# Expert weights that follow the shared weights chunk by chunk, gelu rows moved by pairs, whole-row scatter-adds

## The reference

```python
x = x + ((x*ys) @ W0) * d          # ys = cond/sqrt(512), d = rsqrt(ys^2 @ W0^2 + 1e-8); x is 4096 x 512
s = sigmoid([x, cond] @ router_W); top 2 of 8 by s + router_bias; gates = s_sel / sum(s_sel)
shared = (silu(x @ w1) * (x @ w3)) @ w2                       # hidden 1024
routed = sum over the 2 experts of gate * (gelu(x @ W1e) @ W2e)  # hidden 512
x = x + (shared + routed) / 3
```

## Time and profile before

| | |
|---|---|
| median of 3 runs | 1090.85 us (1090.34 to 1093.66) |
| the profiled execution's own time | 1096.81 us |
| its span | 1095.0 us |
| PE busy | 1036.6 us (95%) |
| DVE, ACT, POOL busy | 509.7, 293.2, 350.3 us |
| chain that ended last | PE 85%, DMA 7%, DVE 3%, issue 3% |

### The profile page before, as it was taken

How to read it: one execution, slowest core, us unless ns; L and a number is a source line. 1 busy time by engine, 2 the same in 40 slices (tenths; PEclk the granted TensorE clock), 3 DMA queues, 4 the chain that set the end, 5 groups by cost and what they waited for, 6 DMA issues and landing times.

```text
span 1095.0 us, 14421 instructions
## 1 busy us (share of the span) xinstructions
PE 1036.6 (95%) x4692; PEld 839.7 (77%) x4692; DVE 509.7 (47%) x824; ACT 293.2 (27%) x461; POOL 350.3 (32%) x320
## 2 busy tenths in 40 slices
PE   6999999999999999999999988979999999999993
PEld 5888778888888888888888876767777777777872
DVE  4555466677332433332322134545555555555642
ACT  3222252332322222222111122223332233233330
POOL 2000000001124434433314001346664454554666
PEclk9999999999999999999999999989999999999997
DMA  4667587768768776778525459978779999999764
GB/s 175 195 217 236 199 287 251 264 227 227 291 211 270 238 274 216 249 255 266 209 49 200 61 171 282 296 172 155 140 147 239 206 218 221 228 225 198 142 119 58
DMA packets 172714, 226.77 MB, mean 207 GB/s; under 512 B 29984, under 2 KB 137888, under 8 KB 163552
## 3 DMA queue, kind: packets, MB, share of 16 engines
q1 hardware_dynamic: 59168, 142.22, 39.8%
q0 software_dynamic: 35024, 46.28, 20.7%
q10 hardware_dynamic: 78464, 37.51, 14.3%
HBM read 111.01 MB, written 96.54 MB: 190 GB/s over the span
## 4 chain that ended last, share of the span: by engine, by line
PE 85%; DMA 7%; DVE 3%; issue 3%; ACT 1%; SPq 0%; POOLq 0%; POOL 0%; DVEq 0%
PE banks L525 11%; PE banks L527 10%; PE banks L526 10%; PE banks L464 10%; PE banks L463 10%; PE banks L465 10%; DMA we<-we_d 5%; PE banks L477 5%; PE banks L478 5%; PE banks L479 5%; PE banks L411 3%; PE banks L412 3%; PE banks L413 3%; DMA out<-ys,row 1%; PE banks L443 1%
## 5 line engine op out<-in xcount | busy, mean ns | idle before, releaser
L1168 POOL DMA_INDIRECT out<-ys,row x142 | 226.2, 1593 | 260.7 <-DMA out<-ys,row 137.2
L463 PE MATMUL banks<-xh,w13h 128*128 128x512 f32 x512 | 200.1, 391 | 1.8 <-DVE xl L732 1.8
L465 PE MATMUL banks<-xh,w13l 128*128 128x512 f32 x512 | 199.9, 390 | 0.0
L464 PE MATMUL banks<-xl,w13h 128*128 128x512 f32 x512 | 199.8, 390 | 0.0
L800 DVE SCALAR_TENSOR_TENSOR gm<-sil,banks 128x512 f32<-128x512 f32 x64 | 43.9, 687 | 252.1 <-ACT sil L606 252.1
L525 PE MATMUL banks<-we,xgth 128*128 x284 | 115.1, 405 | 17.5 <-issue 12.4
L606 ACT ACTIVATE sil<-banks 128x512 f32<-128x512 f32 x64 | 38.2, 597 | 320.9 <-PE banks L465 320.9
L525 PE MATMUL banks<-we,hidth 128*128 x284 | 113.2, 399 | 8.0 <-issue 7.8
L463 PEld LDWEIGHTS banks<-xh,w13h 128*128 128x128 f32 x512 | 96.6, 189 | 22.6 <-issue 2.3
L526 PE MATMUL banks<-we,xgth 128*128 x284 | 112.2, 395 | 0.0
L527 PE MATMUL banks<-we,xgtl 128*128 x284 | 112.2, 395 | 0.0
(11 more groups left out here) (156 smaller groups left out, 1462.2 us busy)
## 6 DMA issues: line engine op xcount, KB each, us to landing
we_d<-ehl SPq DMA_DIRECT2D x32, 1024.0 KB, 7.1
hturn<-hid ACTq DMA_DIRECT2D x284, 64.0 KB
xg<-xs_d ACTq DMA_DIRECT2D x136, 128.0 KB
eraw<-expert_w SPq DMA_DIRECT2D x32, 512.0 KB
we<-we_d SPq DMA_DIRECT2D x8, 2048.0 KB
we<-we_d SPq DMA_DIRECT2D x32, 512.0 KB
x1t_d<-x1t SPq DMA_DIRECT2D x8, 1024.0 KB, 8.8
xin<-x1t_d SPq DMA_DIRECT2D x8, 1024.0 KB, 9.5
```

The lines of the kernel that those rows point to most:

```text
L463: pe.matmul(ps[hc % 2][:, :], w_hi, xh[:, j, c, :], start=(c == 0), stop=False)
L464: pe.matmul(ps[hc % 2][:, :], w_hi, xl[:, j, c, :], start=False, stop=False)
L465: last = pe.matmul(ps[hc % 2][:, :], w_lo, xh[:, j, c, :], start=False, stop=(c == DC - 1))
L1168: pool.indirect_dma_start(out_half, IO(row2[:, h, t:t + 1], 0), ys[:, t % RING, h * D // 2:(h + 1) * D // 2], None, compute_op=ALU.add).th ...
```

## The change

1. `w13h` and `w13l` become one buffer `w13[hc, part]` in the same 64 KiB, so that chunk hc has high and low next to each other. Loads 1, 2, 3 and 4 then lie over chunks 0-1, 2-3, 4-5 and 6-7.
2. SP issues loads 1 to 3 as soon as chunks 1, 3, 5 of the last shared block are multiplied (and the load before has landed). Loads 4 to 7 go in parts of 0.5 MB, each waiting for the part before; the last output store stands behind load 4.
3. `move_h` moves two tiles with 4 DMAs, after the odd tile; `hturn` is [2, 4, 2, 128]. TURN_LAG goes from 2 to 3, LAG from 3 to 4. The hold-back for `o_done` is at t = 1.
4. `scatter` is one indirect DMA of whole rows. It waits for tile t-2, and for tile t-1 only when that is of another expert, or when tiles are padding; the count to wait for is a table `wait_for` that DVE works out in 7 small steps (`scatter_waits`, in place of two operations at L1095) and POOL reads into a register.

```diff
-TURN_LAG = 2
+TURN_LAG = 3
-        w13h = sb("w13h", [HC, 2, DC, P], FP32R, 16)
-        w13l = sb("w13l", [HC, 2, DC, P], FP32R, 48)
+        w13 = sb("w13", [HC, 2, 2 * DC * P], FP32R, 16)
-        hturn = sb("hturn", [RING, SUB, P], FP32, 160)
+        hturn = sb("hturn", [2, SUB, PAIR, P], FP32, 160)
...
-            sp.wait_ge(ab_done, HC * NBLK)
-            load_weight(1, first[0], slice(0, 1))
-            store_out(NBLK - 1)
-            weight_loaded(1)
-            for i in range(2, HRING):
+            for i in (1, 2, 3):
+                sp.wait_ge(ab_done, HC * (NBLK - 1) + 2 * i)
                 load_weight(i, first[i // 2], slice(i // 2, i // 2 + 1))
                 weight_loaded(i)
+            sp.wait_ge(ab_done, HC * NBLK)
+            load_in_parts(4, first[2], slice(2, 3))
+            store_out(NBLK - 1)
+            for i in range(5, HRING):
+                load_in_parts(i, first[i // 2], slice(i // 2, i // 2 + 1))
...
-            def move_h(t):
-                act.wait_ge(hid_done, t + 1 + 2)
+            def move_h(m):
+                n = min(PAIR, TILES - m * PAIR)
+                act.wait_ge(hid_done, m * PAIR + n + 2)
                 for g in range(P // Q):
-                    act.dma_start(hturn[g * Q:(g + 1) * Q, t % RING], hid[:, t % RING, g * P:(g + 1) * P]).then_inc(h_moved[t % RING], 16)
+                    act.dma_start(hturn[g * Q:(g + 1) * Q, m % 2, :, 0:n], hid[:, m % 2 * PAIR:m % 2 * PAIR + n, g * P:(g + 1) * P]).then_inc(h_moved[m % 2], 16)
...
-                    if t == 0:
+                    if t == 1:
                         act.wait_ge(o_done, SUB * NBLK)
-                    move_h(t)
+                    if t % PAIR == PAIR - 1 or t == TILES - 1:
+                        move_h(t // PAIR)
...
-                    for h in range(2):
-                        dve.wait_ge(added[h], 16 * (t + 1 - RING))
+                    dve.wait_ge(added[t % 2], 16 * ((t - RING) // 2 + 1))
...
+            def scatter_waits():
+                at, used = cst[0:1, C_TIX:C_TIX + TILES], e8[0:1, 1, E - 1:E]
+                then(dve.tensor_scalar(wait_for[0:1, :], at, 1.0, None, ALU.add))
+                then(dve.tensor_scalar(wait_for[0:1, :], wait_for[0:1, :], 1, 255, ALU.logical_shift_right, ALU.bitwise_and))
+                then(dve.tensor_tensor(same[0:1, 1:TILES], turn_of[0:1, 1:TILES], turn_of[0:1, 0:TILES - 1], ALU.is_equal))
+                then(dve.tensor_scalar(tail[0:1, :], at, used, None, ALU.is_lt))
+                then(dve.tensor_tensor(same[0:1, 1:TILES], same[0:1, 1:TILES], tail[0:1, 1:TILES], ALU.mult))
+                then(dve.tensor_tensor(same[0:1, 1:TILES], wait_for[0:1, 1:TILES], same[0:1, 1:TILES], ALU.subtract))
+                dve.tensor_scalar(wait_for[0:1, 1:TILES], same[0:1, 1:TILES], 16.0, None, ALU.mult).then_inc(waits_done, 1)
...
             def scatter(t):
+                if t > 1:
+                    pool.wait_ge(added[t % 2], 16 * (t // 2))
+                if 0 < t < 3:
+                    pool.wait_ge(added[(t - 1) % 2], 16)
+                elif t:
+                    landed = pool.value_load(wait_for[0:1, t:t + 1], min_val=16, max_val=16 * (TILES // 2 + 2))
+                    pool.wait_ge(added[(t - 1) % 2], landed)
+                    pool.sem_inc(scatter_free, 1)
                 pool.wait_ge(ys_done, t + 1 + 2)
-                for h in range(2):
-                    if t:
-                        pool.wait_ge(added[h], 16 * t)
-                    pool.indirect_dma_start(out_half, IO(row2[:, h, t:t + 1], 0), ys[:, t % RING, h * D // 2:(h + 1) * D // 2], None,
-                                            compute_op=ALU.add).then_inc(added[h], 16)
+                pool.indirect_dma_start(out[:, :], IO(slot[:, t, 0:1], 0), ys[:, t % RING, :], None,
+                                        compute_op=ALU.add).then_inc(added[t % 2], 16)
```

More of the change, by code:

```diff
@@ L109, in shared_moe_kernel @@
         xgt = sb("xgt", [2, DC, P], FP32, 192)
-        row2 = sb("row2", [2, PADDED], INT32, 196)
+        wait_for = sb("wait_for", [TILES], INT32, 196)
+        same = sb("same", [TILES], INT32, 196.5)
+        tail = sb("tail", [TILES], INT32, 197)
         x1tok = sb("x1tok", [BLK // Q, DC, Q], FP32, 168)
@@ L219, in shared_moe_kernel @@
         xgt_done, hid_done, hidt_done = sem("xgt_done"), sem("hid_done"), sem("hidt_done")
-        h_moved = [sem(f"h_moved{k}") for k in range(RING)]
+        h_moved = [sem(f"h_moved{k}") for k in range(2)]
         ys_done = sem("ys_done")
-        halved = sem("halved")
-        added = [sem(f"added{h}") for h in range(2)]
+        waits_done, scatter_free = sem("waits_done"), sem("scatter_free")
+        added = [sem(f"added{j}") for j in range(2)]
         block = ctx.enter_context(nc.Block())
@@ L326, in load_weight @@
                              we_d[bass.ds(e * 4 + i % 2 * 2, 2)].rearrange("h p s n -> p h (s n)").bitcast(FP32)).then_inc(we_in[i % HRING], 16)
+            parts_before = [16 if i < 4 else 0 for i in range(HRING)]
             def load_in_parts(i, e, place):
                 for q in range(4):
-                    sp.dma_start(we[:, bass.ds(place, 1), i % 2, q // 2, q % 2].rearrange("p a c n -> p (a c n)").bitcast(FP32),
-                                 we_d[bass.ds(e * 4 + i % 2 * 2 + q // 2, 1), :, q % 2].rearrange("a p n -> p (a n)").bitcast(FP32)).then_inc(we_in[i % HRING], 16)
-                    sp.wait_ge(we_in[i % HRING], 16 + 16 * (q + 1))
+                    sp.dma_start(we[:, place, i % 2, q // 2, q % 2].rearrange("p a c n -> p (a c n)").bitcast(FP32),
+                                 we_d[bass.ds(e * 4 + i % 2 * 2 + q // 2, 1), :, q % 2].rearrange("a p n -> p (a n)").bitcast(FP32)).then_inc(we_in[i], 16)
+                    sp.wait_ge(we_in[i], parts_before[i] + 16 * (q + 1))
+                parts_before[i] += 64
                 sp.sem_inc(weights_in, 1)
@@ L375, in _ @@
                 for i in (2 * r, 2 * r + 1):
-                    load_in_parts(i, e, place)
+                    load_in_parts(i % HRING, e, bass.ds(place, 1))
             sp.wait_ge(pads_in, 16)
             sp.wait_ge(out_stored, 16 * NBLK)
-            for h in range(2):
-                sp.wait_ge(added[h], 16 * TILES)
+            for j in range(2):
+                sp.wait_ge(added[j], 16 * ((TILES - j + 1) // 2))
         @block.tensor
@@ L461, in up @@
                     for c in range(DC):
-                        w_hi, w_lo = w13h[:, hc, m, c, :], w13l[:, hc, m, c, :]
+                        w_hi, w_lo = (w13[:, hc, k, (m * DC + c) * P:(m * DC + c + 1) * P] for k in range(2))
                         pe.matmul(ps[hc % 2][:, :], w_hi, xh[:, j, c, :], start=(c == 0), stop=False)
@@ L591, in _ @@
                 act.wait_ge(wraw_in[n % 2], 16 * (n // 2) + 16)
-                act.activation(w13h[:, n].rearrange("p m c n -> p (m c n)"), wraw[:, n % 2, :], ACT.Copy).then_inc(w_high, 1)
+                act.activation(w13[:, n, 0, :], wraw[:, n % 2, :], ACT.Copy).then_inc(w_high, 1)
             def w2_high(g):
@@ L776, in _ @@
                 dve.wait_ge(w_high, n + 1)
-                w_hi = w13h[:, n].rearrange("p m c n -> p (m c n)").bitcast(FP32)
-                dve.tensor_tensor(w13l[:, n].rearrange("p m c n -> p (m c n)"), wraw[:, j, :], w_hi, ALU.subtract).then_inc(w_split, 1)
+                dve.tensor_tensor(w13[:, n, 1, :], wraw[:, j, :], w13[:, n, 0, :].bitcast(FP32), ALU.subtract).then_inc(w_split, 1)
             def w2_low(g):
@@ L1066, in turn_h @@
             def turn_h(t):
-                dve.wait_ge(h_moved[t % RING], 16 * (P // Q) * (t // RING + 1))
+                if t % PAIR == 0:
+                    dve.wait_ge(h_moved[t // PAIR % 2], 16 * (P // Q) * (t // RING + 1))
                 if t >= 2:
@@ L1071, in turn_h @@
                 dve.transpose(hidt[:, t % 2].rearrange("p c (a r) -> p a c r", r=Q),
-                              hturn[:, t % RING].rearrange("p a (c n) -> p a c n", n=Q)).then_inc(hturn_done, 1)
+                              hturn[:, t // PAIR % 2, :, t % PAIR].rearrange("p a (c n) -> p a c n", n=Q)).then_inc(hturn_done, 1)
             def take_h(t):
@@ L1093, in _ @@
                     dve.wait_ge(slots_in, 16 * SUB)
-                    for h in range(2):
-                        dve.tensor_scalar(row2[:, h, :], slot[:, :, 0], 2.0, float(h), ALU.mult, ALU.add).then_inc(halved, 1)
+                    scatter_waits()
                 if t > LAG:
@@ L1158, in _ @@
                         load_row(m + XB)
-            pool.wait_ge(halved, 2)
-            out_half = out.rearrange("t (h d) -> (t h) d", h=2)
+            pool.wait_ge(waits_done, 1)
             def scatter(t):
-                pool.wait_ge(ys_done, t + 1 + 2)
-                for h in range(2):
-                    if t:
-                        pool.wait_ge(added[h], 16 * t)
```

(7 more changed lines are left out.)

## The result

The changed kernel takes 1099.16 us (median of 20 runs, 1093.92 to 1102.71), the kernel before 1087.26 (20 runs, 1078.42 to 1093.66). The ratio is 1.0101, with a 95% interval of 1.0083 to 1.0119. The forecast was 1061. The two profiled executions lie closer together, 1100.87 and 1096.81 us, because that of before was 9.5 us over its own median and above all 20 of its runs: the traces show 4 of the 12 us. Most of the 9.5 us can probably be placed.

What follows compares the result with a forecast made beforehand. The prediction took ACT's queue to set most of the expert loop, with the ring of ys near-critical. Gains of 1.5 + 9.1 + 13.8 + 5.6 = 30.0 us, taken from the median 1090.85, gave 1061 us; 8-in-10 range 1050 to 1076.

Steps and rivals of the forecast that it cites:

- What bounds the kernel now: Expert phase and end: 61 us within reach; ACT's 10.85 us per two tiles against PE's 10.88 sets most of the loop.
- the ring of ys: Second, near-critical loop: beside weight traffic DVE waited 12 times, 15.5 us, for a scatter to land.
- the second stage: Expert phase from 676.2 to 730.9 us: 16 products, 43.5 us of work, in 54.7 us, so 11.2 lost.
- The gelu rows by pairs: Loop of 57 tiles: four fewer ACT issues per two tiles give 5.53 us a tile, 13.8 us gained.
- The unknown that I bounded: ACT's issue of a move with twice the rows: taken as 0.62 us, bounds 0.50 and 0.92.
- The scatters and the weight loads: Second stage: parallel scatters, fewer POOL issues and 0.5 MB parts give 5.7 us a tile, 9.1 us gained.
- the 5 that I put beside it: Second stage: some 5 us gained in place of 9 if load size does not hold back scatters and only the shallower wait helps.
- The start: First tiles: an earlier tile 2 against a later first matmul2 and more DVE work, 1.5 us gained, bounds -2 and 5.
- The tail: Padding tiles and end: whole-row scatters step at 4.6 us and one product moves back, 5.6 us gained, bounds 8 and 1.
- A: Rival on ACT's issues: a paired move costs twice a single one, 1.25 us, so 1106 us, slower; chance 0.06.
- B: Rival on the steady loop: DMA holds it or the issue is near 0.9, so 13.8 shrinks to 2: 1073 us; chance 0.14.
- D: Rival on the scatter: whole rows land in over 5.5 us alone and the ring still fills under traffic: 1070 us; chance 0.1.

Runs made afterwards that it cites:

- e8: The kernel before with load_pair's four issues moved behind the x split of the next iteration: 1.0023 of the kernel before, 1088.06 us.
- e9: The changed kernel with the old half-row scatters and load_pair's issues behind the next iteration's x split: 1.0006 of the kernel before, 1088.02 us.
- e4: The changed kernel with load_pair's four issues behind the x split of the next, even iteration instead of before it: 0.9824 of the kernel before, 1069.76 us.
- e10: The kernel before with one register read per tile instead of two: 1.0036 of the kernel before, 1090.44 us.
- W: Points 1 and 2 of the change (weight layout and loads); put alone into the kernel before: 0.9916 of it, 1080.68 us.
- S: Point 4 of the change (whole-row scatter); put alone into the kernel before: 1.0027 of it, 1092.23 us.
- e1: The kernel before with the whole-row scatter alone: 1.0027 of the kernel before, 1092.23 us.
- e12: e4 with the old weight layout and 2 MB loads taken back: 0.9876 of the kernel before, 1073.88 us.
- the later load: The edit of e4: load_pair's four issues stand behind the next iteration's x split; in the changed kernel 0.9824 of the kernel before.
- e2: The kernel before with the paired moves and lags 3 and 4 alone: 1.0103 of the kernel before, 1100.62 us.
- e7: The changed kernel with one register read per tile instead of two: 0.9972 of the kernel before, 1083.38 us.

## Why the prediction was wrong, step by step

**What bounds the kernel now** was half right. ACT's 10.85 us a pair was a bound, but the ring of ys, called "near-critical", was as much of one (e8, e9). The 11.2 us lost in the second stage and the 17.9 at the end were read from a profile that was long in just these two places.

**The gelu rows by pairs: the step that failed.** "The tight path is the odd tile: from the end of matmul1(t) gelu, four issues, split, DVE's split [...] It fits with 0.7 to spare." The unknown that I bounded was fine: an issue of 128 KB took 0.647 us instead of 0.624, and a pair landed in 4.8 us (8.4 at most). The path itself went on. Behind the h split stand the four token loads, then the x split of tile t+2: from the start of the gelu 854.43 to matmul1 at 862.74 that is 8.3 us, and PE has three products, 8.2 us, there. Over the 28 odd tiles from 13 to 67 it is 8.3 on average and never under 7.96. I had added ACT's work up to a sum per pair and compared it with PE's, and looked at one path through the odd iteration, not at the second. With that split just in time, PE's sequencer loses its lead and the register reads, which I had left at 0.09 us a tile, show as stops of up to 1.0 us every second tile, 13.5 us in all. Forecast 13.8 gained, measured 7.9 lost, which is 22 of the 35 us between the forecast and the trace; with the order mended (e4) 15.8 gained (329.0 to 313.2).

**The scatters and the weight loads.** 6.3 gained in this stage, 9.1 forecast, and that it came so close is mostly luck. The stop near 720 us is gone, and DVE no longer waits for a scatter. But the stop belongs more to that one profile than to the kernel. Here it is, the first line, and the longest stop of PE in that stretch in e10, which keeps the old loads and scatters, the second (in e8 it is 2.60 us):

```profile
722.69 0.79 PE L525 MATMUL banks<-we,xgth 128*128 x1 [5.46 <-issue]
...
723.98 0.49 PE L525 MATMUL banks<-we,xgth 128*128 x1 [1.64 <-issue]
```

The profile of before also shows the granted clock at its lower level (1.2 GHz) for 6.8 us from 721.4, behind that stop; in e8 and e10 the clock is at the full level in the whole stage. So of the 6.3 us some 5 are probably not the change's. W alone took 10.6 us off the first 13 tiles, S alone 4.7, but e8 and e10, with neither, took 5.5 and 5.8.

The loads landed up to 4 us earlier than forecast, the last store went out 8 us earlier (660 for 668), and the parts ended near 736 for 738.

The Trainium skill, "DMA: Bandwidth & Descriptors", section on queues, rings and completion order, has each DMA engine go round between its queues by packets, by which the size of a load would not hold back a scatter. The landings speak against it. Whole-row scatters issued between 685 and 712 us, in e1 beside 2 MB loads, then in the changed kernel beside parts of 0.5 MB:

```profile
DMA to landing us min/median/max: 10.1/10.7/10.8
...
DMA to landing us min/median/max: 4.8/7.2/8.4
```

W also moves 6 MB out of this stretch, so the size of the loads is not the only difference. What it is worth in time is small: e12, with 2 MB loads and the new scatter, took 3.3 us more than e4 from tile 0 to 5 and 2.8 more from tile 5 to 13. Neither my 9 nor the 5 that I put beside it is confirmed by that.

**The start.** Forecast 1.5 gained, measured 3.2 lost; the later load takes the stretch from tile 0 to 5 from 29.4 to 24.7 us, so it is the same fault: four token loads ahead of a split.

**The tail.** Forecast 5.6 gained, measured 0.4 lost. The padding tiles step at 5.2 us, not 4.6: 4.4 to landing and 0.8 to the next. Chain of waits, then POOL:

```profile
1074.71 4.36 DMA out<-ys,slot
...
1079.86 4.30 DMA out<-ys,slot
...
1090.17 1.55 POOL L1187 DMA_INDIRECT out<-ys,slot  x1 [3.68 <-DMA out<-ys,slot]
```

From the last scatter's start to the end of the span are 8.5 us; I had taken 5.4. Four steps of 0.6 and these 3.1 are 5.5 of the 6.0 that separate forecast and trace. Against the tails of e8 and e10, which have the old scatters and LAG 3, it is 4 to 5 us that were lost, and not 0.4. Why the end is 8.5 us behind a whole-row scatter and 5.2 behind a half-row one is not settled.

**The rivals.** A came nearest in price (1106 against 1099) and named the place, the odd path, but its cause was wrong, and that its price came near is luck: a paired move costs 0.647 us and not 1.25. What took the time was the order of the issues, not their size. B's DMA is out. D's condition, more than 5.5 us to land alone, was not met (4.4), but with steps of 5.2 us and a later end a part of its loss came, and its ring did not fill.

What stays open: the parts of the kernel as changed multiply to 1.0045 and it measures 1.0101, a difference at the edge of the noise. If it is real, the stops say where it may lie (13.5 us in mid product against 7.4 in e2 and 9.4 in e1), and e7 shows that without the second register read these stops go.

## What to carry to other kernels

When work is batched on an issuing engine, the sum of its work falls but its longest stretch grows: follow every result that is issued behind the batch, for two iterations, not only the batch's own. Where two resources hold a loop at nearly the same period, a part tested alone can show nothing of what it is worth; test it with the other one freed. The kernel with both holders freed (e4) is the fastest that adds every row, at 0.982 of the one before. Before a stop is priced, see that it is in a second profile too, above all when the profiled execution is slower than every timed run.

## What the runs showed of the hardware

- A register read on PE's queue (TENSOR_LOAD) takes 0.30 us, but up to 1.2 in the changed kernel and 1.6 before. Between 730 and 1035 us the two reads of a tile sum to 0.76 (odd) and 0.82 us (even) before, and to 0.99 in odd tiles of the changed kernel and 1.20 with S alone. In the same stretch, reads that began 2 to 3 us after the start of the last whole-row scatter averaged 0.67 us (33 of them) in the changed kernel and 0.82 (24) in e1; the others averaged 0.31 and 0.34. This is a coincidence in time in two traces, not an experiment.
- ACT's issue of a SBUF to SBUF move doesn't grow with its size here: 0.624 us for 64 KB, 0.647 for 128 KB.
- A whole-row accumulating scatter (256 KB) lands in 4.3 to 8.7 us in the changed kernel, about 4.4 alone, and in 10.1 to 10.8 us beside the 2 MB loads of e1, and its issue takes POOL 1.55 us, as the half's does. Two half-row scatters side by side move the same bytes with steps of 4.46 us; one whole step takes 5.2.
